# Expert weight splits of a two-layer adaLN/FFN/MoE kernel all put on GpSimd, with reordered loads and a sigmoid stage in six pieces

## The chip, the cores and the metric

The kernel runs on one core of one Trainium2 chip. The metric is the device time of one execution in microseconds (us), as a median over runs. Engines are called as in the profile: PE is TensorE, DVE is VectorE, ACT is ScalarE, POOL is GpSimd, SP is SyncE, which here only issues DMAs.

## What is computed

Tokens are 16 batches x 128 steps, 2048 in all, of width 128. The reference, cut to what matters:

```python
x = x + L0_ffn(L0_cond(x, cond))      # modulated linear layer, then a quantised gated FFN of width 384
x = x + L1_ffn(L1_cond(x, cond))      # RNN over 128 steps, then top-2 of 8 experts, each 128 -> 512 -> 128

def L0_ffn(x):                        # act_qdq: scale = max|x| / 32767 over the whole tensor, round to it
    x = act_qdq(x)
    up, gate = act_qdq(x @ dq(w_up).T), act_qdq(x @ dq(w_gate).T)
    sig = round_to_16_bits(sigmoid(gate))
    gate = act_qdq(gate * sig)
    o = act_qdq(gate * up)
    return o @ dq(w_down).T           # dq: 4-bit weights with a scale per block of 32
```

Each `act_qdq` needs the largest absolute value of a whole tensor before its first element can be rounded, so the first layer is a row of stages with a global maximum between them. The second layer's expert weights w1 and w2 are used as two f16 halves (high and low part), which the kernel makes itself.

## The kernel before

The program is written by hand: each engine has its own instruction list, and semaphores connect them. No scheduler changes the order, so an instruction that waits holds up everything written behind it on its engine. The time line of a run has two parts. Up to about 114 us the first layer runs, together with the preparation of the expert weights. From there to the end (352.7 us) a loop over five chunks of tokens and pairs of experts runs; the change doesn't touch it.

The first part, in stages, with the names that the diff uses:

* **Loads.** SP issues w_cond, cond, four pieces of x, w_x and w_h of the RNN, small vectors (`misc`) and then w1 and w2. ACT issues the three FFN weights (`ld_gate`, `ld_up`, `ld_down`).
* **FFN weights.** For gate, up and down in turn (n = 0, 1, 2) DVE makes block scales (`weight_scales(n)`, L592 to L595), POOL rounds the weights with four instructions (L333 to L336), PE turns them (`transpose_weights(n)`, placed ahead of matmul group `W0_AT[n]`), ACT takes the high half and DVE the low half (`weight_lo(n)`, L601). Before this POOL waits for w_x and w_h and splits w_x (L320 to L326).
* **Gate and up.** 24 groups of three matmuls (3 column blocks x 4 token blocks, gate first), each copied out by ACT (L451). DVE takes the maximum of each token block (L632, 1,536 elements in a row, eight times). `peak_to_scale(i)` then makes the global scale: a short DVE reduce (L552), a PE broadcast (`spread_peak`), and four short DVE instructions (L557 to L560). `rw`, `rw_hi` and `rw_lo` are the router's weights, split by DVE (L648 to L650).
* **Sigmoid.** The gate tensor is 6 x 1024 elements in a row and partition. ACT rounds it (L461) and takes the sigmoid (L463); DVE rounds the sigmoid (L637), multiplies (L657) and takes the maximum (L564). There are four pieces, of 1, 1, 2 and 2 sixths.
* **Product.** Up is rounded by ACT (L467), and by POOL where POOL multiplies (L345). Of the six products DVE makes 0, 2 and 4 (L669), POOL 1, 3 and 5 (L348, L349; `P_POOL`), and DVE takes all the maxima (L564).
* **Down.** In five chunks DVE quantises the product and takes its high byte (L680, L682), ACT takes the low byte (L485), PE multiplies by w_down, and DVE makes the layer's output x1 and its halves (`make_x1`: L688, L692, L694). From chunk 2 on PE and ACT also make 16 steps of the RNN, one after the other (L829 and L496); the first needs the halves of x1's chunk 0.
* **Expert weights.** There are 16 chunks of 128x512. A split of a chunk makes an f16 high half and an f16 low half of `wnat` in a buffer, and SP then turns the pair by a transposing DMA (L285) into `wt`. Eight buffers are used twice: four lie in `nat`, four in the memory of `wyT`, which is also the accumulator `acc` of the expert part. So ACT's first copy into `acc` (L507) waits for the transposes of chunks 8 to 11 (`wt_t[2]`):

```python
for k in range(NK):
    first_step(EARLY_STEPS + k)
    act.wait_ge(x1T_mm, k + 1)
    if k == 0:
        act.wait_ge(wt_t[2], 64)
    A(acc[:, 4 * k:4 * k + 4, :].rearrange("p j h -> p (j h)"), banks[ACC_BANKS[k]][:, :],
```

Chunks 0 to 7 are split by POOL with three instructions (L320, L321, L322) after the FFN weights. Of chunks 8 to 15 ACT makes the high half (L405) during the product stage, and DVE the low half (L708) at the end of the down stage.

## Time and profile before

| what | value |
|---|---|
| median of 3 runs | 351.78 us (351.67 to 352.82) |
| profiled execution: its own time | 354.47 us |
| profiled execution: span of the engines | 352.7 us |
| busy: PE, DVE, ACT, POOL | 75%, 89%, 61%, 44% of the span |
| end of the gate and up maxima | 44.0 us |
| end of the sigmoid stage | 65.6 us |
| end of the product stage | 83.3 us |
| first step of the RNN on PE | 94.1 us |
| first matmul with expert weights | 114.1 us |

Busy shares are means over stages with different limits. The last five lines are read off the trace in order of time, from the start of the span, and divide the first layer into the stages of which the text speaks.

### The profile page before, as it was taken

Reading aid. Unit: us, or ns where it says so; the run is one execution under the profiler, and the core shown is the slowest. Engines: PE = TensorE matmul, PEld = TensorE weight load, DVE = VectorE, ACT = ScalarE, POOL = GpSimd, SP = SyncE. Lnnn points to the kernel's source line nnn. Section 1 sums busy time; section 2 is a strip of 40 time slices with the busy share of each in tenths; the row PEclk is TensorE's granted clock in tenths of the full one; section 3 lists DMA queues with packets and bytes.
Section 4 is the critical chain, followed back from the end, with each engine's and each line's share of the span. In section 5 each row is a group of like instructions: output and inputs, shape, how many; then the busy total and the mean of one; then the engine's idle time right before and its main releaser. Section 6 shows DMA issues by size and latency. Waiting matters only on the chain.

```text
span 352.7 us, 8394 instructions
## 1 busy us (share of the span) xinstructions
PE 263.1 (75%) x2587; PEld 191.2 (54%) x2587; DVE 313.4 (89%) x648; ACT 215.3 (61%) x429; POOL 156.4 (44%) x186
## 2 busy tenths in 40 slices
PE   3778440002994996998779999788999989786894
PEld 3633140001454874787457777565777666563683
DVE  4798999897993889789999899999889999999985
ACT  5378898381523775576446676565667655584592
POOL 1459953494020147104771116786110766629500
PEclk9999865555797899899999999999999999999999
DMA  7963430000048000000000000000001000001000
GB/s 209 320 218 62 90 89 0 0 0 0 0 51 189 3 0 0 0 3 18 0 0 0 2 2 25 1 0 0 0 2 32 0 0 0 3 1 33 0 2 22
DMA packets 28074, 12.13 MB, mean 34 GB/s; under 512 B 17369, under 2 KB 26898, under 8 KB 28050
## 3 DMA queue, kind: packets, MB, share of 16 engines
q1 hardware_dynamic: 27106, 11.24, 12.9%
q10 hardware_dynamic: 944, 0.59, 0.7%
q8 instruction: 13, 0.21, 0.2%
q14 instruction: 11, 0.09, 0.1%
HBM read 6.58 MB, written 1.05 MB: 22 GB/s over the span
## 4 chain that ended last, share of the span: by engine, by line
PE 37%; DVE 37%; issue 13%; POOL 5%; DMA 2%; ACT 2%; DVEq 2%; SPq 0%; ACTq 0%; POOLq 0%
PE bank L829 36%; DVE big L804 8%; DVE big L808 5%; DVE wyT L764 5%; DVE peak L632 3%; DVE peak L564 3%; DVE big L657 2%; POOL big L349 2%; POOL big L348 2%; DMA x_sb<-in_x 2%; DVE big L637 1%; DVE big L680 1%; DMA wt<-wyT 1%; DVE big L682 1%; DVE c L688 1%
## 5 line engine op out<-in xcount | busy, mean ns | idle before, releaser
L829 PE MATMUL bank<-wt,big 128*128 (+1 forms) x1536 | 115.8, 220 | 25.1 <-DVE big L808 15.7
L808 DVE TENSOR_TENSOR big<-big 128x384 f16<-128x384 f32 (+2 forms) x160 | 123.2, 777 | 9.9 <-ACT big L527 5.8
L829 PEld LDWEIGHTS bank<-wt,big 128*128 128x128 f16 x1536 | 97.1, 98 | 60.6 <-issue 37.4
L525 ACT ACTIVATE big<-bank,miscT 128x384 f32<-128x384 f32 (+2 forms) x160 | 96.4, 603 | 43.5 <-PE bank L829 39.3
L829 PE MATMUL bank<-big,wt 128*128 128x384 f16 (+2 forms) x480 | 110.4, 339 | 0.0
L360 POOL CAST big<-q 128x64 f16<-128x64 f32 x32 | 10.8, 339 | 128.6 <-ACT q L519 101.6
L804 DVE CAST big<-big 128x512 f16<-128x512 f32 (+2 forms) x112 | 57.3, 512 | 11.2 <-ACT big L525 10.0
L519 ACT ACTIVATE q<-bank,miscT (+1 forms) x112 | 30.7, 274 | 41.8 <-PE bank L829 40.4
L829 PEld LDWEIGHTS bank<-big,wt 128*128 (+1 forms) x480 | 46.6, 117 | 12.4
L829 PE MATMUL bank<-q,wxh 128*128 (+1 forms) x254 | 45.3, 254 | 5.4 <-ACT q L496 5.1
L829 PEld LDWEIGHTS bank<-q,wxh 128*128 128x128 f32 x254 | 39.5, 196 | 10.6 <-ACT q L496 7.0
L764 DVE SCALAR_TENSOR_TENSOR wyT<-bank,gates,wyT 128x128 f32<-128x128 f32 x128 | 39.6, 342 | 0.3 <-issue 0.2
L370 POOL TENSOR_TENSOR big<-big 128x512 f32<-128x512 f32 (+1 forms) x32 | 37.3, 1166 | 2.5
L368 POOL TENSOR_TENSOR big<-b_all,gates 128x1024 f32<-128x1024 f32 x16 | 33.2, 2076 | 7.9 <-issue 7.7
L829 PE MATMUL bank<-ident,pk 128*128 128x128 f32 x10 | 3.2, 415 | 40.0 <-DVE pk L552 40.0
L527 ACT ACTIVATE big<-bank,miscT 128x384 f16<-128x384 f32 (+2 forms) x48 | 28.4, 592 | 0.0
L829 PEld LDWEIGHTS bank<-ident,pk 128*128 128x128 f32 x10 | 2.1, 262 | 41.6 <-DVE pk L552 34.9
L829 PE MATMUL bank<-q,wT_hi 128*128 128x512 f16 x48 | 15.0, 380 | 3.0 <-DVE q L622 2.4
L451 ACT ACTIVATE big<-bank 128x512 f32<-128x512 f32 x24 | 13.9, 604 | 5.0 <-PE bank L829 4.5
L362 POOL TENSOR_TENSOR big<-q,big 128x64 f16<-128x64 f32 x32 | 14.5, 454 | 2.6
L564 DVE TENSOR_REDUCE peak<-big 128x1 f32<-128x1024 f32 (+1 forms) x10 | 14.3, 1433 | 1.2 <-POOL big L349 0.9
L632 DVE TENSOR_REDUCE peak<-big 128x1 f32<-128x1536 f32 x8 | 14.0, 1745 | 0.2
(139 smaller groups left out, 294.0 us busy)
## 6 DMA issues: line engine op xcount, KB each, us to landing
wnat<-in_w SPq DMA_DIRECT2D x8, 512.0 KB, 7.4
x_sb<-in_x SPq DMA_DIRECT2D x4, 256.0 KB, 5.9
out_block<-wyT SPq DMA_DIRECT2D x16, 64.0 KB
b_all<-in_b SPq DMA_DIRECT2D x1, 512.0 KB, 4.8
wn<-in_w_gate ACTq DMA_DIRECT2D x1, 192.0 KB, 2.8
wn<-in_w_up ACTq DMA_DIRECT2D x1, 192.0 KB, 4.5
wn<-in_w_down ACTq DMA_DIRECT2D x1, 192.0 KB, 5.1
wt<-wyT SPq DMA_TRANSPOSE x8, 3.4
```

Source lines behind the costliest of these rows:

```text
L362: G.tensor_tensor(h_lo[:, at], h32[:, at], h_hi[:, at], ALU.subtract).then_inc(h_lo_done, 1)
L368: link(G.tensor_tensor(b2_prod, b2_all[:, :, :], gate, ALU.mult))
L370: link(G.tensor_tensor(b2_prod[:, 0:n, :], b2_prod[:, 0:n, :], b2_prod[:, n:2 * n, :], ALU.add))
L519: A(h32[:, bass.ds(step * B, B)], ps_rnn[:, bass.ds(rnn_column(c, step), B)], ACT.Tanh, bias=bias_h, scale=1 / WS).then_inc(h32_done, 1)
L525: A(g32[:, f, 0:w], ps_h[f][:, 0:w], ACT.Gelu, bias=bias, scale=1 / WS).then_inc(g32_done, 1)
L527: A(g_hi[:, s // NF, f, 0:w], ps_h[f][:, 0:w], ACT.Gelu, bias=bias, scale=1 / WS).then_inc(g_hi_done, 1)
L564: link(V.tensor_reduce(peak[:, i, n:n + 1], t, X, ALU.max, apply_absolute_value=True))
L632: link(V.tensor_reduce(peak[:, i, k:k + 1], tokens((gate2, up2)[i - 1], k), XY, ALU.max, apply_absolute_value=True))
L764: V.scalar_tensor_tensor(a, ps_y[par][:, P * j:P * (j + 1)], g, a, ALU.mult, ALU.add).then_inc(added, 1)
L804: V.tensor_copy(g_hi[:, par, f, 0:w], g32[:, f, 0:w]).then_inc(hi_v, 1)
L808: V.tensor_tensor(g_lo[:, par, f, 0:w], g32[:, f, 0:w], g_hi[:, par, f, 0:w], ALU.subtract).then_inc(g_lo_done, 1)
L829: return nc.tensor.matmul(o, l, r, start=start, stop=stop, skip_group_check=True)
```

## The change

The diff does these things:

* All 16 chunks of the expert weights are split by POOL, in four places of its list: chunks 0 to 6, then 7 and 8, 9 and 10, and 11 to 15. The high halves on ACT and the low halves on DVE go away. The router's split moves from DVE to POOL.
* `weight_scales(1)` moves on DVE from between the quantised x blocks to right behind `weight_scales(0)`, and the maxima of c are put in another order. `weight_lo(2)` moves back by four maxima, the third weight transpose on PE from group 9 to group 14, `spread_peak(1)` from group 19 to 21.
* The loads of w_up and w_down move from ACT's list to SP's, behind x and ahead of w_x; ACT's load of w_gate waits for w_cond and cond.
* The sigmoid stage has six pieces of one sixth. Piece 3 is multiplied by POOL (its three instructions: L347, L349, L350 of the new file), and DVE takes its maximum behind that of piece 4.
* POOL multiplies two products (1 and 3) instead of three; DVE takes their maxima behind those of pieces 2 and 5.

```diff
-W0_AT = (0, 6, 9)
+G2_POOL = (3,)
+W0_AT = (0, 6, 14)
...
-W_POOL = 8
...
-        P_POOL, PEAK_AFTER = (1, 3, 5), (2, 4, 5)
+        P_POOL, PEAK_AFTER = (1, 3), (2, 5)
...
+            sp.dma_start(wn[:, NJ:2 * NJ, :], w_up.rearrange("(j p) i -> p j i", p=P)).then_inc(ld_up, 16)
+            sp.dma_start(wn[:, 2 * NJ:NW, :], w_down.rearrange("p (j i) -> p j i", j=NJ)).then_inc(ld_down, 16)
...
-                if i < W_POOL:
-                    sp.wait_ge(nat_done, i + 1)
-                else:
-                    sp.wait_ge(w_lo_v, i - W_POOL + 1)
+                sp.wait_ge(nat_done, i + 1)
...
+            def split_weights(first, to):
+                for i in range(first, to):
+                    if i % 4 == 0:
+                        pool.wait_ge(ld_w[i // 4], 32)
+                        if i >= 8:
+                            pool.wait_ge(wt_t[i // 4 - 2], 64)
+                    split(nat_of(i)[:, 0:FF], nat_of(i)[:, FF:2 * FF], wnat[:, i % 2, i // 2, :]).then_inc(nat_done, 1)
...
-            for i in range(W_POOL):
-                if i % 4 == 0:
-                    pool.wait_ge(ld_w[i // 4], 32)
-                split(nat_of(i)[:, 0:FF], nat_of(i)[:, FF:2 * FF], wnat[:, i % 2, i // 2, :]).then_inc(nat_done, 1)
+            pool.wait_ge(misc_sb, 1)
+            link(G.tensor_scalar(rw[:, :], miscT[:, SLOTS + 1:NM], WS, 0.0, ALU.mult, ALU.add))
+            link(G.tensor_scalar(rw_hi[:, :], rw[:, :], 1.0, 0.0, ALU.mult, ALU.add))
+            G.tensor_tensor(rw_lo[:, :], rw[:, :], rw_hi[:, :], ALU.subtract).then_inc(rw_done, 1)
+            split_weights(0, 7)
+            for n in G2_POOL:
+                pool.wait_ge(sig_done, n + 1)
+                link(G.tensor_scalar(sixth(gate2, n), sixth(gate2, n), 1.0, -MAGIC, ALU.mult, ALU.add))
+                pool.wait_ge(sig_round, n + 1)
+                link(G.tensor_scalar(sixth(sig2, n), sixth(sig2, n), 65536.0, -SIG_MAGIC * 65536.0, ALU.mult, ALU.add))
+                G.tensor_tensor(sixth(sig2, n), sixth(gate2, n), sixth(sig2, n), ALU.mult).then_inc(g2_pool, 1)
+                pool.wait_ge(g2_pool, 1)
+            split_weights(7, 9)
...
+            split_weights(9, 11)
...
+            pool.wait_ge(p_pool, len(P_POOL))
+            split_weights(11, W_CHUNKS)
...
-            def weight_hi(i):
-                if i % 4 == 0:
-                    act.wait_ge(ld_w[i // 4], 32)
-                    act.wait_ge(wt_t[i // 4 - 2], 64)
-                A(nat_of(i)[:, 0:FF], wnat[:, i % 2, i // 2, :], ACT.Copy, scale=WS).then_inc(w_hi_s, 1)
...
+            act.wait_ge(ld_cond, 32)
...
-            act.dma_start(wn[:, NJ:2 * NJ, :], w_up.rearrange("(j p) i -> p j i", p=P)).then_inc(ld_up, 16)
-            act.dma_start(wn[:, 2 * NJ:NW, :], w_down.rearrange("p (j i) -> p j i", j=NJ)).then_inc(ld_down, 16)
...
-            for n in range(SIG_PIECES):
-                A(piece(gate2, n), piece(gate2, n), ACT.Copy, scale=sc[:, 1, 4:5], bias=MAGIC).then_inc(gateq, 1)
+            for n in range(2 * NJ):
+                A(sixth(gate2, n), sixth(gate2, n), ACT.Copy, scale=sc[:, 1, 4:5], bias=MAGIC).then_inc(gateq, 1)
...
-                A(piece(sig2, n), q16(piece(gate2, n)), ACT.Sigmoid, scale=sc[:, 1, 2:3]).then_inc(sig_done, 1)
+                A(sixth(sig2, n), q16(sixth(gate2, n)), ACT.Sigmoid, scale=sc[:, 1, 2:3]).then_inc(sig_done, 1)
...
-                else:
-                    for m in range(2):
-                        weight_hi(W_POOL + 2 * (n - 3) + m)
-            for i in range(W_POOL + 6, W_CHUNKS):
-                weight_hi(i)
...
+            def scale_c(k):
+                dve.wait_ge(c_mm, k + 1)
+                V.tensor_tensor(c32[:, 4 * k:4 * k + 4, :], batches(banks[k][:, :]),
+                                nrm[:, 1, 4 * k:4 * k + 4].unsqueeze(2).to_broadcast([P, 4, P]), ALU.mult).then_inc(c_v, 1)
+            def peak_c(k):
+                dve.wait_ge(*((c_s, C_SCALAR.index(k) + 1) if k in C_SCALAR else (c_v, k // 2 + 1)))
+                block_peak(0, k, c32[:, 4 * k:4 * k + 4, :].rearrange("p b l -> p (b l)"))
...
-            for k in range(NK):
-                if k in C_SCALAR:
-                    dve.wait_ge(c_s, C_SCALAR.index(k) + 1)
-                else:
-                    dve.wait_ge(c_mm, k + 1)
-                    V.tensor_tensor(c32[:, 4 * k:4 * k + 4, :], batches(banks[k][:, :]),
-                                    nrm[:, 1, 4 * k:4 * k + 4].unsqueeze(2).to_broadcast([P, 4, P]),
-                                    ALU.mult).then_inc(c_v, 1)
-                    dve.wait_ge(c_v, k // 2 + 1)
-                block_peak(0, k, c32[:, 4 * k:4 * k + 4, :].rearrange("p b l -> p (b l)"))
+            weight_scales(1)
+            peak_c(0)
+            scale_c(1)
+            peak_c(1)
+            scale_c(3)
+            peak_c(2)
+            peak_c(3)
...
-                if k == 0:
-                    weight_scales(1)
...
-                link(V.tensor_scalar(piece(sig2, n), piece(sig2, n), SIG_MAX, SIG_MAGIC, ALU.min, ALU.add))
+                V.tensor_scalar(sixth(sig2, n), sixth(sig2, n), SIG_MAX, SIG_MAGIC, ALU.min, ALU.add).then_inc(sig_round, 1)
...
-                    if i == 1 and k == 2:
+                    if i == 2 and k == 2:
...
-                        dve.wait_ge(misc_sb, 1)
-                        link(V.tensor_scalar(rw[:, :], miscT[:, SLOTS + 1:NM], WS, None, ALU.mult))
-                        link(V.tensor_scalar(rw_hi[:, :], rw[:, :], 1.0, None, ALU.mult))
-                        link(V.tensor_tensor(rw_lo[:, :], rw[:, :], rw_hi[:, :], ALU.subtract))
...
-            for n in range(SIG_PIECES):
+            def multiply_sigmoid(n, done):
+                dve.wait_ge(sig_round, n + 1)
+                V.tensor_tensor(sixth(sig2, n), q16(sixth(gate2, n)), q16(sixth(sig2, n), U16), ALU.mult).then_inc(g2_done, 1)
+                dve.wait_ge(g2_done, done)
+                block_peak(3, n, sixth(sig2, n))
+            done = 0
+            for n in range(2 * NJ):
...
-                V.tensor_tensor(piece(sig2, n), q16(piece(gate2, n)), q16(piece(sig2, n), U16), ALU.mult).then_inc(g2_done, 1)
-                dve.wait_ge(g2_done, n + 1)
-                block_peak(3, n, piece(sig2, n))
-            peak_to_scale(3, SIG_PIECES, lambda u: link(V.tensor_scalar(u, sc[:, 1, 2:3], 1.0 / 65536.0, None, ALU.mult)))
+                if n in G2_POOL:
+                    continue
+                done += 1
+                multiply_sigmoid(n, done)
+                if n - 1 in G2_POOL:
+                    dve.wait_ge(g2_pool, G2_POOL.index(n - 1) + 1)
+                    block_peak(3, n - 1, sixth(sig2, n - 1))
+            peak_to_scale(3, 2 * NJ, lambda u: link(V.tensor_scalar(u, sc[:, 1, 2:3], 1.0 / 65536.0, None, ALU.mult)))
...
-            def split_lo(i):
-                dve.wait_ge(w_hi_s, i - W_POOL + 1)
-                V.scalar_tensor_tensor(nat_of(i)[:, FF:2 * FF], wnat[:, i % 2, i // 2, :], WS, nat_of(i)[:, 0:FF], ALU.mult,
-                                       ALU.subtract).then_inc(w_lo_v, 1)
-            for i in range(2):
-                split_lo(W_POOL + i)
...
-            for i in range(2, 4):
-                split_lo(W_POOL + i)
...
-            for i in range(4, W_CHUNKS - W_POOL):
-                split_lo(W_POOL + i)
...
-                if n == NJ * NK + 7:
+                if n == NJ * NK + 9:
...
+                if c == 0:
+                    pe.wait_ge(rw_done, 1)
```

On POOL, from the last chunks split in a row to the last product. `wnat` is the loaded weight, `nat` and `wyT` are the split's buffers, `big` holds gate, up and sigmoid. Before, the list reads (the line with x3 is the rounding of three pieces of up):

```order
L320 TENSOR_SCALAR wnat<-wnat 128x512
L321 TENSOR_SCALAR nat<-wnat 128x512
L322 TENSOR_TENSOR nat<-wnat,nat 128x512
L345 TENSOR_SCALAR big<-big 128x1024 x3
L348 TENSOR_SCALAR big<-big 128x1024
L349 TENSOR_TENSOR big<-big 128x1024
```

In the changed program the same stretch reads, from the sigmoid piece (L347 to L350) on, to the first product:

```order
L347 TENSOR_SCALAR big<-big 128x1024
L349 TENSOR_SCALAR big<-big 128x1024
L350 TENSOR_TENSOR big<-big 128x1024
L313 TENSOR_SCALAR wnat<-wnat 128x512
L314 TENSOR_SCALAR nat<-wnat 128x512
L315 TENSOR_TENSOR nat<-wnat,nat 128x512
L313 TENSOR_SCALAR wnat<-wnat 128x512
L314 TENSOR_SCALAR wyT<-wnat 128x512
L315 TENSOR_TENSOR wyT<-wnat,wyT 128x512
L356 TENSOR_SCALAR big<-big 128x1024 x2
```

Three instructions on the sigmoid and six of splits now stand ahead of the rounding of up, and six more, of chunks 9 and 10, stand between that rounding and the first product (L360, L361). Behind the second product come fifteen more, of chunks 11 to 15.

On DVE, at the end of the down stage (`c` is x1, `x_sb` its halves), the list before is:

```order
L704 CAST big<-big 128x48x24
L708 SCALAR_TENSOR_TENSOR wyT<-wnat,wyT 128x512 x2
L688 SCALAR_TENSOR_TENSOR c<-bank,pk,xT 128x512
L692 CAST x_sb<-c 128x512
L694 TENSOR_TENSOR x_sb<-c,x_sb 128x512
L708 SCALAR_TENSOR_TENSOR wyT<-wnat,wyT 128x512 x2
L688 SCALAR_TENSOR_TENSOR c<-bank,pk,xT 128x384
L692 CAST x_sb<-c 128x384
L694 TENSOR_TENSOR x_sb<-c,x_sb 128x384
L708 SCALAR_TENSOR_TENSOR nat<-wnat,nat 128x512 x4
```

and of the change:

```order
L718 CAST big<-big 128x48x24
L702 SCALAR_TENSOR_TENSOR c<-bank,pk,xT 128x512
L706 CAST x_sb<-c 128x512
L708 TENSOR_TENSOR x_sb<-c,x_sb 128x512
L702 SCALAR_TENSOR_TENSOR c<-bank,pk,xT 128x384
L706 CAST x_sb<-c 128x384
L708 TENSOR_TENSOR x_sb<-c,x_sb 128x384
```

The eight low halves (L708 of before) are gone from between and behind the last two parts of x1.

## Rows read from the trace of the kernel before

**Rows 1.** The page's busy row, and POOL's busy tenths in slices of 8.8 us.

```profile
PE 263.1 (75%) x2587; PEld 191.2 (54%) x2587; DVE 313.4 (89%) x648; ACT 215.3 (61%) x429; POOL 156.4 (44%) x186
POOL 1459953494020147104771116786110766629500
```

**Rows 2.** Chain that ended last, 103 to 114 us: start us, us, what.

```profile
103.80 1.37 DVE wyT L708 x2
105.17 0.82 SPq L285
...
106.04 3.34 DMA wt<-wyT
...
109.45 0.60 ACT wyT L507
```

**Rows 3.** Timeline of the gate and up stage: start us, us, what, idle before it.

```profile
20.29 0.88 POOL L333 TENSOR_TENSOR wn<-wn,ws 128x384 f32<-128x384 f32 x1 [5.92 <-DVE ws L595]
24.65 1.70 DVE L632 TENSOR_REDUCE peak<-big 128x1 f32<-128x1536 f32 x1
31.99 0.85 DVE L648 TENSOR_SCALAR rw<-miscT 128x8 f32<-128x8 f32 x1
```

**Rows 4.** Timeline around the first weights and the first scale.

```profile
10.01 0.30 POOL L320 TENSOR_SCALAR wxh<-wxh 128x128 f32<-128x128 f32 x1 [8.10 <-DMA wxh<-in_w_h]
15.01 0.49 ACT L434 ACTIVATE wT_hi<-bank 128x384 f16<-128x384 f32 x1 [2.03 <-PE bank L864]
15.46 0.15 DVE L554 TENSOR_SCALAR sc<-sc 128x1 f32<-128x1 f32 x1
```

**Rows 5.** Timeline of GpSimd's last split pieces and DVE beside them.

```profile
43.58 0.62 POOL L321 TENSOR_SCALAR nat<-wnat 128x512 f16<-128x512 f32 x1
44.28 1.16 POOL L322 TENSOR_TENSOR nat<-wnat,nat 128x512 f16<-128x512 f32 x1
44.49 1.50 DVE L637 TENSOR_SCALAR big<-big 128x1024 f32<-128x1024 f32 x1
49.56 0.69 DVE L637 TENSOR_SCALAR big<-big 128x1024 f32<-128x1024 f32 x1
50.29 1.23 DVE L657 TENSOR_TENSOR big<-big 128x1024 f32<-128x1024 int16 x1
50.37 2.00 ACT L463 ACTIVATE big<-big,sc 128x2048 f32<-128x2048 int16 x1
58.71 1.55 DVE L637 TENSOR_SCALAR big<-big 128x2048 f32<-128x2048 f32 x1
```

**Rows 6.** Timeline of the product stage, and one quantise instruction behind it.

```profile
69.83 1.22 DVE L564 TENSOR_REDUCE peak<-big 128x1 f32<-128x1024 f32 x1
70.79 2.35 POOL L349 TENSOR_TENSOR big<-big 128x1024 f32<-128x1024 f32 x1
71.09 3.13 DVE L669 TENSOR_TENSOR big<-big 128x1024 f32<-128x1024 int16 x1
73.11 2.01 POOL L348 TENSOR_SCALAR big<-big 128x1024 f32<-128x1024 f32 x1
81.93 1.04 POOL L352 TENSOR_SCALAR b_all<-b_all 128x1024 f32<-128x1024 f32 x1
82.07 1.22 DVE L564 TENSOR_REDUCE peak<-big 128x1 f32<-128x1024 f32 x1 [0.92 <-POOL big L349]
88.31 1.01 DVE L680 TENSOR_SCALAR big<-big,sc 128x1536 f32<-128x1536 f32 x1
```

**Rows 7.** Busy time, granted clock (PEclk) and DMA by stretch, 108 to 120 us.

```profile
core 0: us, PE busy (x) PEld busy (x) DVE busy (x) ACT busy (x) POOL busy (x), PEclk, DMA share, GB/s
108.00:110.00 2.00, 0.00 (x0) 0.00 (x0) 1.32 (x3) 0.55 (x2) 0.00 (x0) 0.97 0.91 191
112.00:114.00 2.00, 2.00 (x10) 1.32 (x10) 0.00 (x0) 1.21 (x3) 0.54 (x2) 0.50 0.85 190
118.00:120.00 2.00, 2.00 (x29) 1.90 (x28) 1.90 (x13) 1.76 (x7) 0.74 (x2) 1.00 0.01 4
```

More of the change, by code:

```diff
@@ L142, in program @@
         pk_part, pk_all, scale_done, dve_step, pool_step = sems("pk_part pk_all scale_done dve_step pool_step")
-        gu_mm, gu_sb, gateq, upq, sig_done, g2_done, p_pool, g2q, p_done, oq, o_hi_done, o_lo_done, o_lo_v = sems(
-            "gu_mm gu_sb gateq upq sig_done g2_done p_pool g2q p_done oq o_hi_done o_lo_done o_lo_v")
+        gu_mm, gu_sb, gateq, upq, sig_done, sig_round, g2_done, g2_pool, p_pool, g2q, p_done, oq, o_hi_done, o_lo_done, o_lo_v = sems(
+            "gu_mm gu_sb gateq upq sig_done sig_round g2_done g2_pool p_pool g2q p_done oq o_hi_done o_lo_done o_lo_v")
         down_mm, x1_done, x1_hi_done, x1_lo_done, x1T_mm = sems("down_mm x1_done x1_hi_done x1_lo_done x1T_mm")
-        nat_done, small_w, w_hi_s, w_lo_v = sems("nat_done small_w w_hi_s w_lo_v")
+        nat_done, small_w, rw_done = sems("nat_done small_w rw_done")
         rnn_mm, h32_done, h_hi_done, h_lo_done = sems("rnn_mm h32_done h_hi_done h_lo_done")
@@ L190, in sixth @@
             return t[:, TOK // 2 * n:TOK // 2 * (n + 1)]
-        SIG_FROM = (0, 1, 2, 4, 6)
-        SIG_PIECES = len(SIG_FROM) - 1
-        def piece(t, n):
-            return t[:, TOK // 2 * SIG_FROM[n]:TOK // 2 * SIG_FROM[n + 1]]
         def tokens(t, k):
```

## The prediction

> **What bounds the kernel now.** I read the busy shares first: DVE is busy 89% of the span, and GpSimd 44%, with long holes in slices 6, 8 and 9 [rows 1]. Work moved onto GpSimd therefore looks free; the question is whether it is free where it is put. The change leaves the expert loop alone, so the first 114 us decide, and I read the chain of waits and the timeline there. Gate and up end at 44.0, the sigmoid stage at 65.6, the product stage at 83.3; the first RNN step starts at 94.1 and the expert matmuls at 114.1. In each of the first three a global maximum closes the stage, and DVE sits on the chain nearly throughout. Behind them the reader is to see a hole: DVE splits chunks 10 and 11 until 105.17, SP issues the transpose, the DMA lands at 109.4, and only then does ACT copy into the accumulator [rows 2]. ACT had nothing else left to wait for from about 104.2. The hole is 5.2 us.
>
> **How GpSimd and DVE share.** This carries the forecast. L349 on GpSimd runs from 70.79 to 73.14. DVE's product L669, issued at 71.09, ends at 74.22, that is 1.08 us after L349's end, though alone such a product takes 1.23. GpSimd's next, L348, issued at 73.11, ends at 75.12, 0.90 after DVE's end, against 1.04 alone [rows 5, 6]. So the two don't slow each other, they take turns, whole instruction by whole instruction. DVE's L637 behind L322 shows the same for a one-input f32 instruction: 1.50 instead of 0.69, and L322 ended at 45.44 [rows 5]. The maxima (1.22) keep their length beside GpSimd. The Trainium skill (SBUF — State Buffer, "SBUF: two separate sides") says that one engine holds the shared ports for a whole instruction and the other fully blocks; by that rule, the trace agrees.
>
> **The change, part by part** (old time to new, all from the profiled execution).
>
> *Front and gate/up: -2.1.* The second set of weight scales leaves the place behind the first q block, where DVE spent 1.2 us on it, and GpSimd no longer idles 5.9 us for it [rows 3]; its cover is DVE's wait for c. PE then doesn't wait for the weights at group 6, and the 24 groups run closely. GpSimd's start has a risk: it waits for w_h, which landed at 10.0, and DVE's L554 ended at 15.61 while ACT's high half came at 15.50, so the slack is 0.1 us [rows 4]. In the new order w_up and w_down stand ahead of w_x on SP. The bytes ahead of it are the same, but nothing but w_cond flows until x starts. Bound: 0 to +1.2; I take +0.4, near the lower end since the bytes are unchanged. The Trainium skill (Trainium Kernel Development and Optimization, "Key Constraints") says that DMAs from SP and ACT run on the same 16 DMA engines and interleave; by that alone this term would be 0.0 and the sum 0.4 lower. The first maximum then starts at 23.5 instead of 24.65 (1.2 earlier by the scales, 0.3 by no collision with the weights on GpSimd, 0.4 later). The router's split, 31.99 to 33.65, goes from DVE: 1.6 off. Waits for ACT's copies give 0.6 back. Maxima end at 44.0 - 1.15 - 1.6 + 0.6 = 41.9. On GpSimd the router's split takes less than 1 us and seven chunks at 2.4 us (0.62 + 0.62 + 1.16, [rows 5]) end near 46.
>
> *Sigmoid stage: 23.1 instead of 21.6, +1.5.* ACT needs 6 x 2.3 us from about 37.6 and is done by 52, ahead of DVE, as it is now (52.4, [rows 5]). DVE has six roundings (0.69 + 0.03), five products (1.26), six maxima (1.25) and 1.5 of scale work: 4.3 + 6.3 + 7.5 + 1.5 = 19.6. Waits: it meets the last split at the first product (0.4), GpSimd's first sigmoid instruction (0.8), its second at piece 4 (0.8), waits for GpSimd's product (1.0), and meets the splits behind it (0.9): 3.9, of which 0.4 is hidden overhead. One product (1.23) less buys four waits. End: 41.9 + 23.1 = 65.0 against 65.6.
>
> *Product stage: 24.7 instead of 17.7, +7.0.* GpSimd can't begin the rest of its piece before DVE's fourth rounding. That ends 12.9 us into the stage (four roundings 2.9, three products and three maxima 7.5, scale work 1.5, waits 1.0), at 54.8. From there to its first product it has, in order: 1.04 + 2.35 for the sigmoid piece, two chunks 4.8, two roundings of up 2.08, two chunks 4.8, 1.04 + 2.35 for product 1 [rows 5, 6]: 18.5, and 18 gaps of 0.08 make 19.9. In that time DVE runs seven roundings and products, each of which stops GpSimd for part of its length; lined up one by one they cost 4.5. Product 1 is ready at 54.8 + 24.4 = 79.2. DVE gets its scale 1.9 after 65.0, at 66.9; its scaling (0.76) and two products with their maxima (5.0) and some 1.7 of stops bring it to 74.4, and there it waits 4.8. Behind it stand four maxima and two products, 7.5, and the two products fall behind GpSimd's own second product and the split of chunk 11 (2.2 + 1.1, 0.3 of it hidden): 79.2 + 10.5 = 89.7, where now the last maximum starts at 82.07 [rows 6] and ends at 83.3. Lower bound of the term: no stops at all, product 1 at 54.8 + 19.9 = 74.7 and the end at 82.2, which is -0.4 for the stage and not +7.0. Upper: every one of the seven in full, 7.3 instead of 4.5, +9.8. I take the middle one because rows 6 show full turns.
>
> *Quantise and down, to the first RNN step: +3.5.* DVE now does L680 and L682 without GpSimd beside it. In the change five chunks, 15 instructions or 12.0 us, and L352 (1.04) stand behind GpSimd's second product, from 82.8 on (79.2 + 3.4 and gaps). By DVE's new scale at 91.7 (89.7 + 2.0) chunks 11 to 13 are through; six instructions and L352 are left, and eight of DVE's ten have to let one pass: 0.2 to 0.9 each, 4.5 with 1.0 hidden. No row shows L680 beside GpSimd; the nearest is L637, the same kind, which a running GpSimd instruction held up (1.55 at 58.71 with 2048 elements, [rows 5]). If it didn't collide, the term would be 0; L680 alone takes 1.01 for 1536 elements [rows 6].
>
> *RNN steps to expert loop: -6.0.* Chunks 8 to 11 are split by 86 and turned by 91, so the 5.2 us hole goes, and DVE's four low halves ahead of the last x1 (0.8 of the chain) go too [rows 2]. What is late next is the row of 16 RNN steps, 0.8 us each, which PE already keeps now.
>
> *Clock: -1.7.* In the hole PE is idle, and the granted clock falls from 0.97 to 0.50, the lower level, and stays there to 117 [rows 7]. With no hole the start of the expert loop runs at the upper level. The 4.3 us from 112.8 on would halve at most to 2.1; the RNN steps within them don't: 1.7. Bounds 0 and 2.1.
>
> Sum: -2.1 + 1.5 + 7.0 + 3.5 - 6.0 - 1.7 = **+2.2**, so the profiled 354.47 becomes 356.7. The profiled execution is 2.7 above the median of the runs, which has nothing to do with the change; on the median, 351.78 + 2.2 = **354.0 us**. A difference under about 0.3% (1 us) can't be told from none.
>
> **Rivals.**
> *Faster: GpSimd gets through in time.* Place: the product stage. If product 1 is ready before DVE has done 0 and 2 (74.4), the wait goes. Speaks for it: 19.9 us without stops reach 74.7, which is close. Against it: the turns of rows 6. At half of the price of the product and quantise terms (+3.5, +1.7) the sum is -2.1 + 1.5 + 3.5 + 1.7 - 6.0 - 1.7 = -3.1: 348.7 us. The break-even is at 8.3 us for the two terms together, where I have 10.5. Chance 0.26.
> *No difference.* The same with three quarters of the price: 351.3 us, chance 0.13.
> *Worse: the front loses too, and the clock isn't kept.* w_h lands 1.2 later, and PE waits for x1 at 99 to 103, long enough to lose the upper level: 2.2 + 0.8 + 1.7 = +4.7, 356.5 us. For it: slack of 0.1 [rows 4]; against: the RNN steps keep PE at work from 103 on. Chance 0.16.
> The forecast, slower by 1.1 to 3.9 (352.9 to 355.7), has 0.45.
>
> **How the numbers follow.** Faster 0.26, within 0.3% 0.13, slower 0.45 + 0.16 = 0.61. The range takes in the faster case at 348.7 and the worse case at 356.5 with a little room for its upper bound (+9.8 instead of 7.0 in part): 348.5 to 357.5.
>
> **What would show it.** In the new profile: gate and up maxima end near 42; GpSimd has no hole between 55 and 100; DVE idles about 5 us in the product stage with GpSimd's product as releaser; the stage ends near 90; L694 and L696 of the new file (the quantising pair) are longer than 1.01 and 0.96; ACT doesn't wait for the transposes; the clock is 1.00 at the start of the loop, which begins 2 to 4 us later than 114. I am wrong if DVE's wait for product 1 is under 2 us, or if chunks 13 to 15 are split before 90.

## The result and the profile after

The changed kernel takes 359.82 us (median of 4 runs, 359.13 to 361.49), the kernel before 352.30 in the 4 runs beside it (351.67 to 353.23): ratio 1.0218, 95% interval 1.0174 to 1.0263. It is slower, as forecast, but by 7.5 us instead of 2.2, and outside the range.

The profiled executions differ by less: 359.13 against 354.47, +4.7. The first lines to read are the busy row and GpSimd's tenths, which answer to [rows 1]:

```profile
PE 261.6 (73%) x2587; PEld 190.1 (53%) x2587; DVE 313.1 (88%) x643; ACT 211.7 (59%) x425; POOL 177.8 (50%) x213
POOL 1739927999941117312883014877110666619500
PEclk9879865555589999899999999999999999999999
```

GpSimd now works without a hole in slices 7 to 11 (54 to 98 us) and DVE has no less to do (313.1 against 313.4 us): what DVE gave away it pays back in longer instructions. The clock row has an 8 and a 7 in slices 2 and 3 (9 to 27 us), ahead of gate and up and at their start.

The stages. The first three end at the short DVE reduce that stands 0.03 us behind their last maximum; the others end at the first RNN step on PE, at the start of the input matmul ahead of the expert loop, and at the end of the span. The last two columns are a second profile of either kernel, unchanged (below):

| stage, us | before | forecast | after | before again | after again |
|---|---|---|---|---|---|
| gate and up end at | 44.05 | -2.1 | 42.62 (-1.4) | 44.25 | 41.05 |
| sigmoid stage | 21.59 | +1.5 | 22.87 (+1.3) | 21.59 | 22.94 |
| product stage | 17.68 | +7.0 | 24.76 (+7.1) | 17.68 | 24.76 |
| to the first RNN step | 10.76 | +3.5 | 14.58 (+3.8) | 10.76 | 14.50 |
| to the input matmul | 18.70 | -6.0 | 14.23 (-4.5) | 18.74 | 14.30 |
| to the end | 239.9 | -1.7 | 238.3 (-1.6) | 238.2 | 238.2 |

Timeline of the changed kernel, DVE and GpSimd (start us, us, what, idle before and releaser), against [rows 5] and [rows 6]:

```profile
40.85 1.74 DVE L639 TENSOR_REDUCE peak<-big 128x1 f32<-128x1536 f32 x1
...
60.16 1.22 DVE L565 TENSOR_REDUCE peak<-big 128x1 f32<-128x1024 f32 x1 [1.05 <-POOL big L350]
...
73.89 1.22 DVE L565 TENSOR_REDUCE peak<-big 128x1 f32<-128x1024 f32 x1
79.80 1.22 DVE L565 TENSOR_REDUCE peak<-big 128x1 f32<-128x1024 f32 x1 [4.69 <-POOL big L361]
81.06 3.16 DVE L683 TENSOR_TENSOR big<-big 128x1024 f32<-128x1024 int16 x1
...
99.15 1.90 DVE L694 TENSOR_SCALAR big<-big,sc 128x1536 f32<-128x1536 f32 x1
101.08 1.68 DVE L696 TENSOR_SCALAR big<-big 128x1536 f16<-128x1536 int8 x1
```

The wait of 1.05 is the one for GpSimd's sigmoid product (I had 1.0), that of 4.69 the one for product 1 (4.8). L683 beside GpSimd's product takes 3.16, alone 1.23. And the quantising pair is longer than alone: 1.90 for the 1.01 of [rows 6], and 1.68 for an int8 conversion that takes 0.96 alone (in e3_tiny_late below). Here is GpSimd ahead of product 1 and beside the quantising pair, where before it had nothing to do:

```profile
74.42 0.62 POOL L314 TENSOR_SCALAR wyT<-wnat 128x512 f16<-128x512 f32 x1
75.12 1.15 POOL L315 TENSOR_TENSOR wyT<-wnat,wyT 128x512 f16<-128x512 f32 x1
76.24 1.04 POOL L360 TENSOR_SCALAR big<-big 128x1024 f32<-128x1024 f32 x1
77.36 2.34 POOL L361 TENSOR_TENSOR big<-big 128x1024 f32<-128x1024 f32 x1
...
96.00 1.13 POOL L313 TENSOR_SCALAR wnat<-wnat 128x512 f32<-128x512 f32 x1
97.21 1.20 POOL L314 TENSOR_SCALAR nat<-wnat 128x512 f16<-128x512 f32 x1
98.50 1.73 POOL L315 TENSOR_TENSOR nat<-wnat,nat 128x512 f16<-128x512 f32 x1
100.20 1.75 POOL L366 TENSOR_SCALAR b_all<-b_all 128x1024 f32<-128x1024 f32 x1
```

Product 1 starts right behind chunk 10. Chunk 15 ends at 100.2; its three instructions take 4.2 us instead of 2.4. The 1.90 of L694 is beside its last one; the 1.68 of L696 is beside L366, the bias scaling behind it, which takes 1.75 here and 1.04 alone. PE at its two weak places, which the forecast had wrong:

```profile
5.08 5.54 PE L830 MATMUL bank<-x_sb,wyT 128*128 128x128 f32 x32
...
14.58 0.55 PE L865 MATMUL bank<-ident,wn 128*128 128x128 f32 x3 [2.27 <-POOL wn L329]
...
19.20 0.59 PE L830 MATMUL bank<-q,wT_hi 128*128 128x512 f16 x1 [2.43 <-DVE q L631]
...
104.23 0.37 PE L830 MATMUL bank<-x_sb,wx_hi 128*128 128x256 f16 x1 [5.06 <-DVE x_sb L708]
```

The same stretches by windows (busy us of each engine, granted clock PEclk, DMA share, GB/s):

```profile
12.00:16.00 4.00, 1.73 (x14) 1.50 (x13) 2.85 (x8) 0.49 (x1) 3.58 (x7) 0.94 1.07 353
16.00:20.00 4.00, 1.57 (x6) 0.72 (x5) 2.54 (x8) 2.16 (x4) 1.34 (x2) 0.50 1.09 373
20.00:24.00 4.00, 4.00 (x15) 1.59 (x14) 3.60 (x9) 3.45 (x7) 0.68 (x1) 0.71 0.68 237
...
104.00:108.00 4.00, 3.77 (x16) 2.45 (x17) 3.26 (x6) 0.55 (x2) 0.00 (x0) 0.57 0.00 0
108.00:112.00 4.00, 4.00 (x27) 2.27 (x26) 2.38 (x4) 1.37 (x5) 0.00 (x0) 1.00 0.01 4
```

At both places PE had idled (2.3 and 2.4 us; 5.1 us), and the clock stands at the lower level, 1.2 GHz, when the work comes: at 16 to 20 and past the middle of 20 to 24, where the gate matmuls start, and at 104 to 107, where the RNN steps start. In the kernel before, the windows from 12 to 28 all read 1.00, although PE waits 2.43 us at 18.50 there too; ahead of its first weights it waits 0.86.

### The profile page after: what moved, and what is told of

It is laid out like the page before. It is cut to its first block, busy times and chain, and to the rows that moved or that the text cites. A ratio compares the mean times of both kernels' runs of the same rounds, so it can differ in the third digit from the quotient of the medians.

```text
span 357.3 us, 8414 instructions
## 1 busy us (share of the span) xinstructions
PE 261.6 (73%) x2587; PEld 190.1 (53%) x2587; DVE 313.1 (88%) x643; ACT 211.7 (59%) x425; POOL 177.8 (50%) x213
## 3 DMA queue, kind: packets, MB, share of 16 engines
HBM read 6.58 MB, written 1.05 MB: 21 GB/s over the span
## 4 chain that ended last, share of the span: by engine, by line
PE 40%; DVE 32%; issue 13%; POOL 8%; ACT 2%; DVEq 2%; DMA 1%; SPq 1%; ACTq 0%; POOLq 0%
PE bank L830 39%; DVE big L805 8%; DVE big L809 5%; DVE wyT L765 5%; DVE peak L639 3%; DVE peak L565 2%; DVE big L683 2%; DVE big L696 2%; POOL wnat L313 1%; DVE big L694 1%; DMA wxh<-in_w_h 1%; DVE big L659 1%; POOL wyT L315 1%; POOL big L350 1%; DVE big L644 1%
## 5 line engine op out<-in xcount | busy, mean ns | idle before, releaser
L830 PEld LDWEIGHTS bank<-big,wt 128*128 (+1 forms) x480 | 46.1, 116 | 12.2
L565 DVE TENSOR_REDUCE peak<-big 128x1 f32<-128x1024 f32 x12 | 14.6, 1220 | 6.1 <-POOL big L361 4.7
L486 ACT ACTIVATE big<-big 128x1536 f16<-128x1536 uint8 (+2 forms) x4 | 5.0, 1244 | 23.7 <-DVE big L694 23.7
L830 PE MATMUL bank<-q,wT_hi 128*128 128x512 f16 x48 | 16.1, 405 | 2.4 <-DVE q L631 2.4
```

The lines of the kernel that those rows point to most:

```text
L565: link(V.tensor_reduce(peak[:, i, n:n + 1], t, X, ALU.max, apply_absolute_value=True))
L830: return nc.tensor.matmul(o, l, r, start=start, stop=stop, skip_group_check=True)
```

## The experiments

All ratios are to the kernel before, whose medians in the three sets were 352.85 (21 runs), 352.66 (19) and 353.49 (15). "Changed kernel" is 359.82; in the last set it took 360.06.

**e1_front: the front part alone** (load order, both weight scales early, router split on GpSimd, W0_AT 14), on the kernel before.

```diff
-W0_AT = (0, 6, 9)
+W0_AT = (0, 6, 14)
...
             weight_scales(0)
-            for k in range(NK):
...
+            weight_scales(1)
+            peak_c(0)
+            scale_c(1)
...
-                if k == 0:
-                    weight_scales(1)
```

> The kernel before with only the front of the change: load order, both weight scales early, the router's split on GpSimd, third weight transpose at group 14, broadcast at group 21. My theory (the front gains and the loss comes later): gate and up maxima end near 42.6 instead of 44.0, and the time is 0.5 to 1.5 us below before, since DVE then meets one split more on GpSimd. Rival (the front itself loses, by the later arrival of w_h): 0 to 1.5 us above before.

Measured: 352.47 us, ratio 0.9974 (0.9942 to 1.0006), with runs from 349.69 to 356.05. Gate and up end at 44.07, where they do without it, and not at the 42.6 expected. Its clock, by windows:

```profile
12.00:16.00 4.00, 1.81 (x10) 1.57 (x11) 2.92 (x7) 0.25 (x1) 3.66 (x6) 0.83 1.03 305
16.00:20.00 4.00, 1.85 (x9) 1.55 (x7) 1.74 (x6) 1.33 (x3) 1.49 (x3) 0.74 1.08 365
20.00:24.00 4.00, 3.68 (x11) 1.35 (x12) 3.86 (x9) 3.72 (x8) 0.00 (x0) 0.68 0.79 274
24.00:28.00 4.00, 4.00 (x20) 1.85 (x18) 1.97 (x3) 2.48 (x5) 2.68 (x4) 0.89 0.00 0
```

What the front saves on DVE, PE seems to lose here at the lower clock (e12_after_again and e5_warm have the same front with the clock at 1.00, and end gate and up at 41.05 and 41.01). The front part doesn't make the kernel slow, and a gain from it can't be told from none.

**e2_pool12: four more weight chunks to GpSimd, nothing else**, on the kernel before. They stand ahead of GpSimd's products, as the first eight do.

```diff
-W_POOL = 8
+W_POOL = 12
...
                     pool.wait_ge(ld_w[i // 4], 32)
+                    if i >= 8:
+                        pool.wait_ge(wt_t[i // 4 - 2], 64)
```

> The kernel before, with chunks 8 to 11 also split by GpSimd directly behind chunk 7, in its idle time of the sigmoid stage; chunks 12 to 15 stay on ACT and DVE. My theory (GpSimd's work is paid by DVE in turns, but place decides): the 5.2 us hole before the expert loop goes, DVE has 0.8 less on the chain, the sigmoid stage is 2.5 to 3.5 longer, the product stage the same: 2 to 4 us below before. Rival (any more split on GpSimd in these stages costs more than the hole): 0 to 3 us above before.

Measured: 347.86 us, ratio 0.9848 (0.9804 to 0.9893), 5.0 us faster than before, more than was expected of it. Sigmoid stage 22.3 (+0.7), product stage 18.4 (+0.7), to the first RNN step 10.75 (+0.0), from there to the input matmul 13.1 instead of 18.7 (-5.6). Its chain of waits, 105 to 113 us, where [rows 2] had DVE's split, SP and a transpose of 3.34:

```profile
105.44 1.35 DVE nat L708 x2
106.79 0.81 DVE c L688
107.60 0.02 issue
107.62 0.37 DVE x_sb L692
108.00 0.02 issue
108.02 0.57 DVE x_sb L694
108.59 0.14 issue
108.72 4.31 PE bank L829 x48
```

The transposes are off the chain: its last piece before PE is the last x1 itself. So the hole, the only large gain of the change, needs chunks 8 to 11 and no more. Chunks 12 to 15 and the regrouped products aren't needed for it.

**e3_tiny_late: chunks 11 to 15 shrunk** to 8 of 512 columns (the rest of these weights isn't split), on the changed kernel.

```diff
+                    n = 8 if 11 <= i < 16 else FF
-                    split(nat_of(i)[:, 0:FF], nat_of(i)[:, FF:2 * FF], wnat[:, i % 2, i // 2, :]).then_inc(nat_done, 1)
+                    split(nat_of(i)[:, 0:n], nat_of(i)[:, FF:FF + n], wnat[:, i % 2, i // 2, 0:n]).then_inc(nat_done, 1)
```

> The changed kernel, with the splits of chunks 11 to 15 cut to 8 columns of 512 (the rest of these weights is left unsplit, that work is left out). My theory (these 15 instructions take turns with DVE's quantising): from the end of the product stage to the first RNN step 10.5 us instead of 14.6, PE isn't idle for 5 us before it, and the time is 3.5 to 5 us below the changed kernel, so 3 to 4 us above before. Rival (turns in this stage cost nothing): within 1 us of the changed kernel.

Measured: 353.49 us, ratio 0.9999 (0.9970 to 1.0027), 6.3 below the changed kernel and more than expected. The profiled execution took 355.59: its clock is 0.50 from 16 to 24 us, and its gate and up end at 44.83; the stages behind can be compared. From the product stage to the first RNN step 10.74 instead of 14.58. The rows, against 1.90 and 1.68 of the changed kernel:

```profile
98.44 1.01 DVE L695 TENSOR_SCALAR big<-big,sc 128x1536 f32<-128x1536 f32 x1
99.49 0.96 DVE L697 TENSOR_SCALAR big<-big 128x1536 f16<-128x1536 int8 x1
```

The whole +3.8 of this stretch is GpSimd's late chunks, and they cost more on either side of it: the product stage is 1.0 shorter (23.8, without chunk 11), and from the first RNN step to the input matmul it takes 12.9 instead of 14.2, since PE waits 0.6 us ahead of that step instead of 5.06 and the clock reads 1.00 from 104 to 108. Together 6.1 us in the stages, beside the 6.3 of the medians.

**e4_tiny_mid: chunks 9 and 10 shrunk** in the same way (`9 <= i < 11`; the rest of these two isn't split).

> The changed kernel, with the splits of chunks 9 and 10 cut to 8 columns of 512 (that work is left out). My theory (they hold up GpSimd's first product, for which DVE waits 4.7 us): the product stage is 4.5 to 5.5 us shorter, the five later chunks start 5 us earlier relative to the stage and meet DVE's quantising about as before, so the time is 4.5 to 7 us below the changed kernel, about before's +1 to +3. Rival (the wait is set by turns, not by the queue): 1 to 2 us below the changed kernel.

Measured: 356.30 us, ratio 1.0098 (1.0068 to 1.0127), 3.5 below the changed kernel. Product stage 21.27 instead of 24.76, with DVE's wait 2.18 instead of 4.69:

```profile
77.34 1.22 DVE L566 TENSOR_REDUCE peak<-big 128x1 f32<-128x1024 f32 x1 [2.18 <-POOL big L362]
```

I had expected 4.5 to 5.5 in the stage. The two chunks took 3.4 and 3.5 us of GpSimd's way; shrunk they still take 2.35 together (0.20 an instruction, and one that meets DVE's product 1.05). The rounding behind them then meets DVE's product and takes 2.10 instead of the 1.04 at 76.24. So product 1 comes 3.5 us earlier in the stage, and the stage is 3.5 shorter. DVE's own two products, with fewer turns to give, are through 1.0 earlier as well, so its wait shrinks by 2.5 only.

**e5_warm: PE kept busy** in its two waits, on the changed kernel.

```diff
                 if k == 1:
+                    for _ in range(36):
+                        mm(banks[5][:, 0:P], ident16[:, :], ident16[:, :], True)
                     transpose_weights(0)
...
                 if c == 2:
+                    for _ in range(80):
+                        mm(banks[7][:, 0:P], ident16[:, :], ident16[:, :], True)
                     pe.wait_ge(small_w, 2)
```

> The changed kernel, with matmuls on PE that nothing reads in its two waits: 36 of 128x128 ahead of the first weight transposes, and 80 ahead of the first RNN step. Nothing else is changed. My theory (PE's new idle times, 2.3 us at 12.3 and 5.1 us at 99, drop the granted clock to the lower level, and the matmuls behind them then set the pace of the front and of the first RNN steps): the granted clock is 1.00 from 16 to 28 us and at 104 to 108, gate and up maxima end 1 to 2 us earlier than in the changed kernel, first RNN steps take 0.8 us, time 2 to 4 us below the changed kernel. Rival (the clock costs nothing, since DVE sets the pace): within 0.7 us of the changed kernel, or above it.

Measured: 357.38 us, ratio 1.0118 (1.0066 to 1.0170), 2.4 below the changed kernel, the two intervals just apart. Gate and up end at 41.01, the first RNN step to the input matmul is 12.93. PE's row at the first weights and the windows at both places:

```profile
14.84 0.55 PE L865 MATMUL bank<-ident,wn 128*128 128x128 f32 x3 [0.21 <-POOL wn L329]
```

```profile
16.00:20.00 4.00, 1.53 (x10) 0.65 (x9) 2.99 (x9) 2.46 (x5) 1.51 (x3) 1.00 1.09 369
20.00:24.00 4.00, 4.00 (x21) 2.00 (x20) 3.90 (x8) 3.92 (x8) 0.88 (x2) 1.00 0.72 252
...
104.00:108.00 4.00, 4.00 (x27) 2.21 (x27) 3.29 (x6) 1.37 (x5) 0.00 (x0) 1.00 0.00 0
```

**e6_wx_later: GpSimd doesn't wait for w_h** before the gate weights; the RNN weights are split behind the second weight set, on the changed kernel.

```diff
-            pool.wait_ge(ld_wx, 32)
-            split(wx_hi[:, :], wx_lo[:, :], wxh[:, 0, :]).then_inc(small_w, 1)
...
                 G.tensor_tensor(wb, wb, scale, ALU.mult).then_inc(wdeq, 1)
+                if n == 1:
+                    pool.wait_ge(ld_wx, 32)
+                    split(wx_hi[:, :], wx_lo[:, :], wxh[:, 0, :]).then_inc(small_w, 1)
```

> The changed kernel, with GpSimd's split of w_x and w_h behind the second FFN weight instead of ahead of the first. My theory (the front doesn't gain because GpSimd waits for w_h until 10.2 and PE for the weight until 14.6): the first weight is ready at about 12.2, PE has no 2.3 us wait there, the first scale comes 1 to 2 us earlier, and the time is 1.5 to 3 us below the changed kernel. Rival (the front is bound by DVE's maxima of c, and the clock drop has another cause): the first scale moves by less than 0.5 us and the time by less than 1.

Measured: 358.79 us, ratio 1.0155 (1.0101 to 1.0208), 1.0 below the changed kernel, which can't be told from none: its four runs reach from 356.51 to 359.98. The first FFN weights are now ready at 10.1:

```profile
9.24 0.83 POOL L323 TENSOR_TENSOR wn<-wn,ws 128x384 f32<-128x384 f32 x1 [7.33 <-DVE ws L597]
```

Gate and up end at 41.52, though the clock is 0.70 at 16 to 20 and 0.87 at 20 to 24: the wait on GpSimd is gone, and PE still runs out of work before the first scale.

**e7_mid_behind: chunks 9 and 10 moved behind the products**, none left out.

```diff
-            split_weights(9, 11)
...
-            split_weights(11, W_CHUNKS)
+            split_weights(9, W_CHUNKS)
```

> The changed kernel, with the splits of chunks 9 and 10 moved behind GpSimd's two products; only the order is changed. My theory (all of GpSimd's work is paid by DVE, so moving it shifts the place of the payment): the product stage is 5 us shorter, from its end to the first RNN step it is 3 to 5 us longer, since six instructions more meet DVE's quantising, and the time is within 2 us of the changed kernel. Rival (the queue ahead of the first product is the whole loss): 4 to 6 us below the changed kernel.

Measured: 355.86 us, ratio 1.0081 (1.0050 to 1.0112), 4.0 below the changed kernel. Product stage 19.74 (-5.0), then 15.41 to the first RNN step (+0.8) where the theory of full payment expected +3 to +5, and 15.26 from there to the input matmul (+1.0). The +1.0 stands where PE's clock is at the lower level (window 100 to 104 at 0.50, 104 to 108 at 0.72), behind a wait of 6.08 us ahead of the first RNN step, and needs no turns. So the cost of the same chunks depends on the place: behind the products part of them runs beside DVE's maxima and its scale work, which neither hold GpSimd up nor are held up (the maxima take 1.22 here too). To move the two chunks gives as much as to leave most of their work out (e4_tiny_mid, 356.30).

**e8_no_g2pool: the sigmoid product stays on DVE.**

```diff
-G2_POOL = (3,)
+G2_POOL = ()
```

> The changed kernel, with all six sigmoid pieces multiplied by DVE. GpSimd then doesn't stand still from 48.2 to 55.4 for DVE's fourth rounding, and splits chunks 7 and 8 there. My theory (the piece costs by its place in GpSimd's list): the sigmoid stage keeps its length within 1 us, GpSimd's first product comes before 72 instead of 79.8, the product stage takes 17 to 19 us instead of 24.8, the time is 5 to 8 us below the changed kernel. Rival (the splits set it whatever is ahead of them): 0 to 3 us below.

Measured: 354.71 us, ratio 1.0038 (1.0001 to 1.0075), 5.1 below the changed kernel. The sigmoid stage gets longer, 24.67 instead of 22.87 (I had expected it within 1 us), and the product stage shorter, 19.03 instead of 24.76. To have one 1.23 us product off DVE saves 1.8 us where it is made and costs 5.7 where GpSimd arrives late for its next one. (The two stages and 0.7 lost in the RNN steps give 3.3 net, the profiled executions 3.8, the medians 5.1.)

**e9_best: the front part, twelve chunks and the later RNN weights** (the edits of e1_front, e2_pool12 and e6_wx_later together), on the kernel before. **e10_best_warm** is e9_best with 32 small matmuls behind the maxima's transposes of the first scale:

```diff
             spread_peak(0)
+            for _ in range(32):
+                mm(banks[5][:, 0:P], ident16[:, :], ident16[:, :], True)
```

> The kernel before with the front of the change, chunks 8 to 11 split by GpSimd directly behind chunk 7, and w_x and w_h split behind the second FFN weight; sigmoid and product stages are those of before. My theory (the front gains once GpSimd doesn't wait for w_h, and the four chunks fill GpSimd's idle time of the sigmoid stage): the gains of both add up, gate and up maxima end near 41.5, 6 to 8 us below before. Rival (DVE, earlier by 2 us, meets more splits, and the front's gain is paid back in the sigmoid stage): 4.5 to 5.5 us below before, as with the four chunks alone.

> The kernel of e9 with 32 matmuls of 128x128 that nothing reads behind the first global maximum, in PE's wait of 2.5 us for the quantised x. My theory (the granted clock fell there for 16 to 24 us in e6): the clock is 1.00 there, and the time 0.5 to 1.5 us below e9. Rival: no difference, since ACT's copies and DVE set the pace.

Measured: e9_best 347.57 us, ratio 0.9838 (0.9816 to 0.9860), 5.9 below the kernel before, between the two expectations; e10_best_warm 346.97, ratio 0.9817 (0.9795 to 0.9840). Against e2_pool12 (347.86 in another set) the front and the later RNN weights add nothing that can be told; keeping PE busy adds 0.6, less than in e5_warm, and the intervals of the two overlap, though gate and up end 1.5 us earlier (40.44 against 41.98). e10_best_warm is the fastest of all, 6.5 us ahead of the kernel before.

**e11_before_again and e12_after_again: both kernels unchanged**, once more.

> The kernel before, unchanged, for a second profile. If the first profile of before was a slow one, as its 354.47 beside the median of 352.7 has it, its expert loop took longer: 238.4 us or less here from the first input matmul to the end, instead of 239.9. If the medians differ from the profiles for another reason, it is 239.9 again.

> The changed kernel, unchanged, for a second profile. If its first profile had a lucky front (clock back at the upper level by 22 us), gate and up maxima end here at 43 to 45 instead of 42.6, and first RNN step and expert loop come later by as much; the product stage has 24 to 25 us and the stretch behind it 14 to 15 again. If the front isn't what varies, 42.6 again.

Measured: 353.45 us, ratio 1.0002 (0.9982 to 1.0021), and 360.06, ratio 1.0211 (1.0179 to 1.0244). Their stages stand in the table above: the four in the middle repeat within 0.1 us. Gate and up of the changed kernel don't (42.62 and 41.05, and 43 to 45 was expected of the second), nor does the last stretch of the kernel before (239.9 and 238.2, as expected of it). In e12_after_again PE waits as in the first profile, yet keeps the upper clock, 2.4 GHz, in the front:

```profile
14.89 0.55 PE L865 MATMUL bank<-ident,wn 128*128 128x128 f32 x3 [2.20 <-POOL wn L329]
```

```profile
16.00:20.00 4.00, 1.53 (x9) 0.68 (x8) 2.94 (x9) 2.41 (x5) 1.56 (x3) 1.00 1.10 369
...
100.00:104.00 4.00, 1.27 (x7) 0.94 (x8) 3.90 (x6) 1.26 (x2) 0.44 (x1) 0.85 0.28 64
104.00:108.00 4.00, 4.00 (x20) 2.31 (x19) 1.79 (x4) 0.89 (x4) 0.00 (x0) 0.72 0.00 0
```

## Why the prediction was right in its direction and wrong in its size

What failed, in the order of its size: the sum took the profiled execution of before for typical, 2.7 us above the median "which has nothing to do with the change", and left out that the granted clock also falls elsewhere in the loop, in some executions and not in others; the term of the RNN steps (-6.0) left out PE's wait ahead of the first of them and measured -4.5; the front (-2.1) came out between 0.0 and -3.2, with PE's clock, which had no part in that term. The terms that carried the forecast held.

**Taking turns: right.** The three terms that rest on it were +1.5, +7.0 and +3.5; measured +1.3, +7.1 and +3.8, together 12.2 instead of 12.0. The steps inside them held too: product 1 ready at 79.7 (79.2), DVE's wait 4.69 (4.8), stage end at 90.2 (89.7). e4_tiny_mid, e7_mid_behind and e8_no_g2pool each shorten GpSimd's way to product 1 and take 3.5 to 5.7 off the product stage; e3_tiny_late takes the late chunks away and gets the 3.8 back. That L694 and L696 collide, for which no row stood before, is shown by their 1.90 beside chunk 15 and 1.68 beside L366 behind it, and 1.01 and 0.96 without GpSimd. The Trainium skill (SBUF — State Buffer, "SBUF: two separate sides") says that one engine holds the shared ports for a whole instruction and the other fully blocks. The trace agrees for these forms, the int8 one as well (1.68 against 0.96); the maxima kept 1.22 throughout.

**Front and gate/up, -2.1: wrong.** Measured -1.4 in the profile of the result (-1.6 against e11_before_again), -3.0 to -3.2 in e12_after_again and 0.0 in e1_front, where I had one number. My step "in the new order w_up and w_down stand ahead of w_x ... I take +0.4" looked at the wrong thing. w_h landed at almost its old time: GpSimd starts on it at 10.17, before at 10.01 [rows 4], so 0.16 and not 0.4. (The Trainium skill, Trainium Kernel Development and Optimization, "Key Constraints", with DMAs of both issuers interleaving on the same 16 engines, gave 0.0 here; the trace is nearer to that.) What moved was x: the matmuls of c now start at 5.08, 1.9 us earlier than before, and PE is through with them when the gate weights, held by GpSimd behind w_h, are still 2.3 us away. In that gap the clock may fall, and then the maxima's transposes and the first gate matmuls run at the lower level. With PE kept busy (e5_warm) they end at 41.0, which is 0.9 better than forecast. DVE's savings are there; whether they arrive depends on PE's clock, which I hadn't looked at for this stage. The wait for w_h isn't the whole reason: e6_wx_later has none, and its clock still reads 0.70 at 16 to 20.

**RNN steps to expert loop, -6.0: right in kind, 1.5 too much.** The hole is gone, as e2_pool12 shows by itself (-5.6). But PE idles 5.06 us ahead of the first RNN step, because DVE, held up by GpSimd's late chunks and by L366, brings x1 late (without these chunks PE waits 0.6, e3_tiny_late), and the window of the first steps reads 0.57. e5_warm keeps PE busy there and gets 12.93, which would be -5.8. This is one half of my rival "worse"; I gave it 0.16 because "the RNN steps keep PE at work from 103 on", and that looked behind the wait instead of ahead of it. The other half of the rival, w_h 1.2 us later, didn't happen (0.16 us).

**Clock, -1.7: right, and hidden by a second fall of the clock that comes and goes.** The last row of the table reads 239.9 and 238.2 for two profiles of the kernel before, and 238.3 and 238.2 for the changed one, so against the second profile the gain seems to be nothing. The windows show why. Two from before, two from e11_before_again, then one each from after and e6_wx_later:

```profile
132.00:140.00 8.00, 5.57 (x60) 4.31 (x58) 7.69 (x14) 4.20 (x13) 5.93 (x8) 1.00 0.00 0
140.00:148.00 8.00, 7.21 (x70) 6.16 (x69) 6.38 (x18) 4.48 (x13) 1.50 (x4) 0.79 0.00 0
132.00:140.00 8.00, 5.57 (x61) 4.35 (x58) 7.69 (x14) 4.22 (x12) 5.94 (x8) 1.00 0.00 0
140.00:148.00 8.00, 7.08 (x78) 5.57 (x77) 7.36 (x21) 5.67 (x16) 1.97 (x6) 1.00 0.00 0
...
140.00:148.00 8.00, 6.35 (x62) 5.17 (x61) 7.62 (x15) 4.32 (x12) 5.65 (x8) 0.83 0.00 0
140.00:148.00 8.00, 6.42 (x74) 5.16 (x71) 7.81 (x16) 5.08 (x15) 4.91 (x6) 1.00 0.00 0
```

From the input matmul to the end, by what the clock does at these two places (the rest of the loop is at 1.00 in all seven, up to its last 3 us):

| us | clock at 1.00 from 140 to 148 | clock falls between 140 and 150 |
|---|---|---|
| loop starts at 0.50, as in the kernel before | 238.2 (e11_before_again), 238.4 (e1_front) | 239.9 (before) |
| loop starts at 1.00, as in the changed kernel | 236.9 (e4_tiny_mid), 236.9 (e6_wx_later) | 238.3 (after), 238.2 (e12_after_again) |

Like with like, the start at the upper level brings 1.3 to 1.7 us, where the forecast had 1.7; 0.5 of it comes before the first expert matmul (0.83 us behind the input matmul instead of 1.34). The second fall costs 1.3 to 1.6. It was in both profiles of the changed kernel and in one of two of the kernel before, with PE equally busy ahead of it. Whether the change makes it more frequent isn't shown.

**The sum.** On the pair of profiles: -1.4 + 1.3 + 7.1 + 3.8 - 4.5 - 1.6 = +4.7, as measured. Here the second fall is on both sides. Against e11_before_again, which at 353.08 is nearer to the medians, the same table gives -1.6 + 1.3 + 7.1 + 3.8 - 4.5 + 0.0 = +6.1, which is 3.9 above the forecast: 0.5 for the front, 0.2 for the turns, 1.5 for the RNN steps, and 1.7 for the clock, whose gain at the start of the loop the second fall takes back. The expert loop so begins at 119.9, 5.8 us later than before, where 2 to 4 was forecast. The other 1.5 us up to the 7.5 between the medians aren't in any trace: the changed kernel's eight executions reach from 357.57 to 361.70, the profiled ones are the fastest of each four, and 353.08 is 0.8 above the median beside the result. Their mean granted clock speaks for more time at the lower level: 0.918 at 357.57 us and 0.909 at 359.13, and 0.900 at both 361.49 and 361.70, though 0.896 goes with 360.61. The two profiles of before differ in the same way, 0.917 at 354.47 and 0.923 at 353.08. That e5_warm is 2.4 below the changed kernel in the median, and 1.1 to 2.6 in the profile, points there as well. For the executions that weren't traced it is argued and not shown.

Not tested alone are the sigmoid stage in six pieces, GpSimd's two products instead of three, and the place of chunks 7 and 8; so how the 7.1 us of the product stage divide over the queue ahead of product 1 is known for chunks 9 and 10 and for the sigmoid piece only.

**What it comes to.** GpSimd's added work costs DVE time wherever both want to run, and it costs most where DVE then waits for GpSimd's product. The useful part was four chunks in GpSimd's idle time ahead of its products, -5.0 us alone.

## What to carry to other kernels

Work moved to GpSimd is hidden only while DVE is in instructions that don't take turns with it (here its maxima and the scale work) or waits for something else; ahead of each product that GpSimd owes DVE, add up its queue with the turns, and place the moved work where the sum stays short of DVE's arrival. Move the part that opens the known hole first, and alone: four chunks gave 5.0 us, all eight with the rest lost 7.5. When a load order or a faster engine brings PE's work forward, look at the wait that then stands in front of PE's next work, because the clock may fall in it. And before a difference of 1 or 2 us between two profiles is put down to a change, or a term is called wrong by it, compare the granted clock window by window over the whole span, and take a second profile of the same kernel.

## What the runs showed of the hardware

The same idle time of PE, 2.2 to 2.3 us behind the matmuls of c and 2.4 behind the transposes, cost the clock in some executions and not in others: 0.50 at 16 to 20 us in the first profile after, 0.74 in e1_front, 1.00 in e12_after_again. Gate and up ended between 41.05 and 44.83 in six executions whose front was the same code. Small matmuls with no use for the result kept it at 1.00 in e5_warm and took 2.4 us off the median. In the expert loop the clock fell in the window from 140 to 148 us in one of two executions of the same program (0.79 and 1.00), with PE busy 5.57 of the 8 us ahead of it in both, and such a fall cost 1.3 to 1.6 us.

Turns are dear for the engine with the shorter instruction: DVE's 1.23 us product took 3.16 beside a 2.34 us one of GpSimd, and GpSimd's 0.62 us scaling took 1.47 and 1.59 beside DVE's products (at 69.37 and 72.74 us). With both queues full, chunks that take 2.4 us alone took 3.4 to 4.2. DVE's maxima took 1.22 us in every case, beside GpSimd or not.
